# A mixture-of-experts block whose second expert stage writes its rows straight to the output

## The reference

```python
def ffn(x_):                                    # x_: 4096 x 128
    idx = argmax(x_ @ router.T, axis=-1)        # one of 8 experts for each token
    y  = down[idx] @ (silu(gate[idx] @ x_) * (up[idx] @ x_))           # 128 -> 256 -> 128
    ys = (silu(x_ @ w_gate_s.T) * (x_ @ w_up_s.T)) @ w_down_s.T        # the shared expert
    return y + ys

x = x + 0.5 * ffn(layernorm(x))
n = layernorm(x)
x = x + n + gate * circ_corr(decayed_sum(circ_conv(n, bind_key)), unbind_key)   # sum over earlier tokens
x = x + 0.5 * ffn(layernorm(x))
```

## Time and profile before

| | |
|---|---|
| median of 3 runs (lowest to highest) | 297.3 us (297.2 to 298.74) |
| the profiled execution | 297.33 us |
| its span | 295.6 us |
| TensorE busy | 254.9 us, 86% |
| TensorE weight loads | 211.0 us, 71% |
| VectorE busy | 189.0 us, 64% |
| ScalarE busy | 160.5 us, 54% |
| GpSimd busy | 178.7 us, 60% |
| mean DMA rate | 96 GB/s |

### The profile page before, as it was taken

One profiled execution on the slowest core, in us unless ns is written; L12 is line 12 of the kernel. 1 busy time (PEld: TensorE's weight loads), 2 busy tenths in 40 slices (PEclk: granted clock), 3 DMA queues, 4 the chain that ended last, 5 costly groups with the idle time before them and its releaser, 6 DMA issues.

```text
span 295.6 us, 6436 instructions
## 1 busy us (share of the span) xinstructions
PE 254.9 (86%) x1788; PEld 211.0 (71%) x1788; DVE 189.0 (64%) x734; ACT 160.5 (54%) x374; POOL 178.7 (60%) x260
## 2 busy tenths in 40 slices
PE   0799999969999999985589988999779999999940
PEld 0557777648999999845466767766369999999520
DVE  4695665864555555448996999867625566565362
ACT  2705545145767767326497877750447767775100
POOL 6555677722777777723457788877307758887400
PEclk9999999999999999997676999999999999999995
DMA  6970111323344321147000001112323434311297
GB/s 187 332 300 27 48 55 59 95 79 74 102 111 107 105 81 47 45 130 185 0 1 27 29 28 38 49 45 83 96 64 104 107 94 111 90 54 48 65 303 237
DMA packets 34996, 28.42 MB, mean 96 GB/s; under 512 B 4784, under 2 KB 31792, under 8 KB 34704
## 3 DMA queue, kind: packets, MB, share of 16 engines
q1 hardware_dynamic: 25328, 16.06, 19.7%
q0 software_dynamic: 4544, 9.45, 9.7%
q10 hardware_dynamic: 5088, 2.50, 2.9%
HBM read 15.37 MB, written 12.62 MB: 95 GB/s over the span
## 4 chain that ended last, share of the span: by engine, by line
POOL 33%; PE 22%; issue 19%; DMA 10%; DVE 9%; ACT 2%; SPq 2%; POOLq 0%; DVEq 0%; ACTq 0%
POOL dispatched L349 15%; POOL returned L378 12%; PE bank L951 10%; PE bank L959 4%; PE bank L874 4%; DMA ey<-returned 4%; POOL scale_f L338 2%; DMA xres<-in_x 2%; POOL token L372 2%; DMA dispatched<-xn,slot 2%; DMA returned<-ey,token 2%; DVE st_f L550 1%; DMA xs<-dispatched 1%; SPq L308 1%; PE bank L899 1%
## 5 line engine op out<-in xcount | busy, mean ns | idle before, releaser
L378 POOL DMA_INDIRECT returned<-ey,token x78 | 76.8, 985 | 32.8 <-issue 17.8
L951 PE MATMUL bank<-xsT,wgu 128*128 128x128 f32 x624 | 83.0, 276 | 2.4 <-ACT xsT L497 2.4
L349 POOL DMA_INDIRECT dispatched<-xn,slot x64 | 63.5, 992 | 24.6 <-issue 17.7
L951 PEld LDWEIGHTS bank<-xsT,wgu 128*128 128x128 f32 x624 | 75.7, 192 | 3.4 <-ACT xsT L497 1.7
L874 PE MATMUL bank<-xnT,gu 128*128 128x512 f32 x128 | 66.7, 649 | 3.6 <-DVE hs L623 2.8
L805 DVE COPY ey<-bank 128x128 f32<-128x128 f32 x78 | 22.7, 292 | 45.6 <-PE bank L959 45.6
L481 ACT ACTIVATE wgu<-gu 128x512 f32 x78 | 48.3, 623 | 4.1 <-issue 3.9
L454 ACT ACTIVATE sg<-bank 128x512 f32<-128x512 f32 x32 | 18.9, 592 | 54.7 <-PE bank L874 47.3
L959 PE MATMUL bank<-wdn,eh 128*128 128x128 f32 x312 | 47.5, 276 | 0.5 <-DVE eh L800 0.5
L503 ACT ACTIVATE eg<-bank 128x256 f32<-128x256 f32 x78 | 29.8, 383 | 32.6 <-PE bank L951 32.4
L959 PEld LDWEIGHTS bank<-wdn,eh 128*128 128x128 f32 x312 | 40.9, 192 | 0.9 <-DVE eh L800 0.9
(11 more groups left out here) (102 smaller groups left out, 282.7 us busy)
## 6 DMA issues: line engine op xcount, KB each, us to landing
xs<-dispatched SPq DMA_DIRECT2D x80, 66.0 KB, 1.9
ey<-returned SPq DMA_DIRECT2D x16, 256.0 KB, 5.7
gu<-in_gu SPq DMA_DIRECT2D x1, 2048.0 KB, 11.3
out<-xres ACTq DMA_DIRECT2D x8, 256.0 KB, 4.2
returned<-ey,token POOLq DMA_INDIRECT x78
dn<-in_dn SPq DMA_DIRECT2D x1, 1024.0 KB, 11.7
dispatched<-xn,slot POOLq DMA_INDIRECT x64, 2.3
dispatched<-pads SPq DMA_DIRECT2D x10, 66.0 KB
```

Of the source, the lines that this page charges most:

```text
L349: nc.gpsimd.indirect_dma_start(dispatched[:, :], bass.IndirectOffsetOnAxis(slot[:, i:i + 1], 0), xn[:, i, :], None, bounds_check=last_row) ...
L378: nc.gpsimd.indirect_dma_start(returned[:, :], bass.IndirectOffsetOnAxis(token[:, b:b + 1], 0), ey[:, b, :], None, bounds_check=last_back) ...
L951: last = nc.tensor.matmul(bank[4 + b % WR][:, i * P:(i + 1) * P], wgu[:, b % WR, i * P:(i + 1) * P], xsT[:, b // 2 % 2, b % 2, :], start=T ...
```

## The change

In stage 1 the dispatched row also carries the residual of its token. `xn` becomes 260 words wide, 132 as before and 128 that are now the storage of `xres`; `dispatched` becomes two tensors, one with rows of 132 words for stage 0 and one with rows of 260 for stage 1. In stage 1 the residual must be complete when it is dispatched, so all 24 shared parts are done before: a front step `k` does (k-1, 1), (k-1, `DOWN`) and (k, 0), there is one more step, `front(1, G)`, and `scatter(1, k-1)` is issued in step k, behind a wait for `half_done` of its group. VectorE does the first of the three parts ahead of `choose`, where it was behind. The evacuation of an expert block in stage 1 multiplies the product by 0.5 and adds the residual that came with the row; the indirect transfer writes to `out`. Rows of padding and repeated blocks are beyond the bound and not written. The read back, sums and stores of stage 1 are gone.

```diff
-    dispatched = nc.dram_tensor("dispatched", [E * CAP, ROW], F32, kind="Internal")
-    returned = nc.dram_tensor("returned", [DUMP * (E + 1), C], F32, kind="Internal")
+    dispatched = [nc.dram_tensor(f"dispatched{f}", [E * CAP, w], F32, kind="Internal")
+                  for f, w in enumerate((ROW, WIDE))]
+    returned = nc.dram_tensor("returned", [N, C], F32, kind="Internal")
+    home = [returned[:, :], out.rearrange("b t c -> (b t) c")]
...
-        xres = sb("xres", [P, NT, C])
-        xn = sb("xn", [P, NT, ROW])
+        xn = sb("xn", [P, NT, WIDE])
+        xres = xn[:, :, ROW:WIDE]
...
-        xs = sb("xs", [P, NBL, ROW])
+        xs = sb("xs", [P, NBL, WIDE])
+        ey = xs[:, :, ROW:WIDE]
+        back = ey
...
-        def parts_at(k, i):
-            return SHARED_PARTS[PER_STEP * (k - 1) + i:][:1] if 1 <= k < G else []
+        def parts_at(f, k, i):
+            if f == 0:
+                return SHARED_PARTS[PER_STEP * (k - 1) + i:][:1] if 1 <= k < G and i < PER_STEP else []
+            g, part = ((k - 1, 1), (k - 1, DOWN), (k, 0))[i]
+            return [(g, part)] if valid(g) and 0 <= k <= G else []
...
             def scatter(f, k):
                 pool.wait_ge(slotted, f * G + k + 1)
+                if f == 1:
+                    pool.wait_ge(half_done, G + k + 1)
                 for i in range(k * TPG, (k + 1) * TPG):
                     nc.gpsimd.indirect_dma_start(
-                        dispatched[:, :], bass.IndirectOffsetOnAxis(slot[:, i:i + 1], 0),
-                        xn[:, i, :], None, bounds_check=last_row).then_inc(sent, 16)
+                        dispatched[f][:, :], bass.IndirectOffsetOnAxis(slot[:, i:i + 1], 0),
+                        xn[:, i, 0:width(f)], None, bounds_check=last_row).then_inc(sent, 16)
...
-                if valid(k):
-                    scatter(1, k)
+                if valid(k - 1):
+                    scatter(1, k - 1)
...
                     nc.gpsimd.indirect_dma_start(
-                        returned[:, :], bass.IndirectOffsetOnAxis(token[:, b:b + 1], 0),
-                        ey[:, b, :], None, bounds_check=last_back).then_inc(blk_out, 16)
+                        home[f], bass.IndirectOffsetOnAxis(token[:, b:b + 1], 0),
+                        ey[:, b, :], None, bounds_check=last_back, oob_is_err=False).then_inc(blk_out, 16)
...
             # ScalarE, front(f, k); PE takes part i = 2 at the very end of its step
-                for g, part in parts_at(k, 1):
-                    shared(f, g, part)
+                for i in (1, 2):
+                    for g, part in parts_at(f, k, i):
+                        shared(f, g, part)
...
             # VectorE, front(f, k)
+                if f == 1:
+                    for g, part in parts_at(f, k, 0):
+                        shared(f, g, part)
                 if valid(k):
                     root = f == 0 and k == 2
                     choose(n, q, kind, later, later, root)
...
                 def evac_y(b):
                     dve.wait_ge(blk_dn, f * NB + b + 1)
-                    nc.vector.tensor_copy(ey[:, b, :], y_of(b)).then_inc(blk_y, 1)
+                    if f == 0:
+                        done = nc.vector.tensor_copy(ey[:, b, :], y_of(b))
+                    else:
+                        done = nc.vector.scalar_tensor_tensor(out=ey[:, b, :], in0=y_of(b), scalar=0.5,
+                                                              in1=ey[:, b, :], op0=ALU.mult, op1=ALU.add)
+                    done.then_inc(blk_y, 1)
...
             steps(middle, 4)
+            front(1, G)
             before_experts(1)
             experts(1)
-            for g, part in SHARED_PARTS[LATE:-1]:
-                shared(1, g, part)
-            for k in range(G):
-                add_back(1, k, x3_done)
-                if k == 2:
-                    shared(1, *SHARED_PARTS[-1])
```

More of the change, by code:

```diff
@@ L25 @@
 ROW = C + 4
+WIDE = ROW + C
 CAP = N + P
@@ L416, in _ @@
             steps(middle, 4)
+            scatter(1, G - 1)
             experts(1)
@@ L484, in before_experts @@
             def before_experts(f):
-                for g, part in SHARED_PARTS[EARLY:LATE - 1]:
+                for g, part in SHARED_PARTS[EARLY:LATE - 1] if f == 0 else []:
                     shared(f, g, part)
@@ L688, in front @@
                             newton_step(i)
-                for g, part in parts_at(k, 0):
-                    shared(f, g, part)
+                if f == 0:
+                    for g, part in parts_at(f, k, 0):
+                        shared(f, g, part)
                 if f == 1 and valid(k + 2):
@@ L907, in front @@
                     last.then_inc(mixed, 1)
-                for g, part in parts_at(k, 1):
+                for g, part in parts_at(f, k, 1):
                     shared(f, g, part)
@@ L929, in front @@
                     turn("a", k + 3, xa, 1 - q, x2_done)
+                for g, part in parts_at(f, k, 2):
+                    shared(f, g, part)
             def count_all():
@@ L965, in experts @@
                 turn_pair(0)
-                pe.wait_ge(half_done, f * G + parts_done(LATE, down=True))
-                pe.wait_ge(mult_done, f * G * HH + parts_done(LATE, down=False))
+                last = PARTS if f else LATE
+                pe.wait_ge(half_done, f * G + parts_done(last, down=True))
+                pe.wait_ge(mult_done, f * G * HH + parts_done(last, down=False))
                 gate_up_block(0)
@@ L997, in _ @@
             steps(lambda k: front(1, k), 3)
-            for g, part in SHARED_PARTS[EARLY:LATE]:
-                shared(1, g, part)
+            front(1, G)
             experts(1)
-            for g, part in SHARED_PARTS[LATE:]:
-                shared(1, g, part)
 def kernel(L0_attn_x, L0_attn_bind_key, L0_attn_unbind_key, L0_attn_gate, L0_attn_decay, L0_ffn_up, L0_ffn_gate,
```

53 lines of the change are left out of this document (25 added, 28 removed).

## The result

The changed kernel takes 310.4 us (median of 6 runs, 309.7 to 314.6), the kernel before 297.4 us on the same chip (6 runs, 296.8 to 299.0): 4.8% slower, ratio 1.048 with a 95% interval of 1.043 to 1.054. The forecast was 307.8 us, within 301 to 315. Executions over 1.5% above the fastest of the same kernel are left out of all ratios, and of the medians in the table of the experiments.

What follows compares the result with a forecast made beforehand. It took the kernel as bound by the stage 2 routing front, then TensorE in the experts, then a 16.8 us tail after the last expert row. Sum: 297.33 + 26.7 (front) + 0.6 (wide rows) - 16.8 (tail) = 307.8 us, range 301 to 315.

Steps and rivals of the forecast that it cites:

- The end: After the last expert row lands: read back, sums and stores go, removing 16.8 us; the last transfer lands in 2.25 us.
- The loop of 10.6 us: Stage 1 front: waits between ScalarE, VectorE and TensorE close a loop, making one full step 10.6 us.
- two changed orders: Stage 1 front: ScalarE's norm ahead of the second silu, VectorE's product ahead of `choose`; together they close the 10.6 us loop.
- The steps one by one: Stage 1 front: gate-up starts from 155.37 us to 224.2 us, the first gate-up at half clock costing 1.74 us.
- step 6: Stage 1 front step without `add_self`: forecast to take 8.2 us.
- the clock rival: Stage 1 front: TensorE's waits drop it to half clock, 312 us, or 318 with gate-ups slow too; chance 0.14.
- The last dispatch at 236.0: End of the front: the last transfer into `dispatched` starts at 236.0 us, was 209.30; the front gets 26.7 us longer.
- Wide rows: Landing and first read of a block: dispatched rows of 1040 bytes, were 528, add 0.6 us, between 0 and 0.9.
- GpSimd's time for wide rows: GpSimd's 0.97 us for each transfer into `dispatched`: taken as unchanged by wider rows, adding nothing.
- that rival: GpSimd pays for wide rows: its 0.97 us rise by half, 309.4 us, or double, 312.8 us; chance 0.08.
- The experts: Second expert stage: multiply-add in place of VectorE's copy out of PSUM, priced at nothing; stage stays at 58 us.
- The packed rival: Stage 1 front: the loop doesn't close, parts pack into idle time, last transfer starts at 226.7; 298.5 us, chance 0.12.

Runs made afterwards that it cites:

- e7: Kernel before with only the end changed: rows straight to the output, padding dropped, no read back, residual or last five shared parts; 283.6 us, ratio 0.953.
- e8: As e7, but rows go to the scratch tensor with none dropped, and the output gets one early store; 282.0 us, ratio 0.949.
- e3: Changed kernel with `choose` put back ahead of the product on VectorE, as before the change; 324.5 us, ratio 1.096.
- e4: Changed kernel with the edits of e2 and e3 together; 319.4 us, ratio 1.079.
- e12: Changed kernel with ten unread TensorE products added ahead of the second expert stage; 309.3 us, ratio 1.042.
- e1: The changed kernel run again, unaltered, for a second profile; 311.2 us, ratio 1.051 to the kernel before.
- e9: e5 with `add_self` moved right behind the norm of `xa` of the step before on ScalarE; 298.2 us, ratio 1.003.
- e2: Changed kernel with the second silu put ahead of `add_self` and the norm on ScalarE in stage 1; 302.9 us, ratio 1.021.
- e6: Changed kernel with two unread 128x512 products added ahead of each gate-up (k-1, 1) of stage 1; 314.5 us, ratio 1.058.
- e5: e2 with VectorE's product of (k-1, 0) moved behind the scan and read-back sum of the next step; 300.9 us, ratio 1.016.
- e10: e9 with ten unread TensorE products added ahead of the second expert stage; 296.9 us, ratio 1.002.
- e11: e10 with gate-up (7, 0) ahead of group 6's down part, and the last down part and sum in halves; 297.1 us, ratio 1.002.

## Why the prediction was right, and where its sizes were off

**The end** (16.8 us removed): right in kind, 2.2 us too large. It took the landing of 2.25 us for all that follows the last transfer; in the changed kernel, e7 and e8 it is 4.4 us, because GpSimd's closing drain ends 2.1 us after the landing. That term was left out of the sum.

**The loop of 10.6 us**: the steps from 154.82 us on measured 10.55, 10.55, 10.55, 10.27 and 9.80 us, where 10.6, 10.6, 10.6, 10.3 and 9.8 were forecast, the half clock apart. Each link was where it was put, to within 0.15 us: silu at + 1.92, second silu + 5.97 for 6.07, product + 6.63 for 6.70, `add_retrieved` and transposes to 10.55. But one sentence behind it was wrong. It said that two changed orders close the loop, and only ScalarE's is shown as a cause; VectorE's product ahead of `choose` is the better order (e3, e4). The links were read rightly; what the old order would cost in their place was never worked out.

**The steps one by one**: the sum from the first gate-up to that of group 7 was forecast as 68.8 us and is 68.8 (154.82 to 223.63), but by two errors that cancel. The half clock was put at the first gate-up, as in the earlier trace rows; in this profile it didn't fall there, and fell at the down product of step 6 in its place (forecast 8.2 us, measured 9.93), with TensorE's clock in these two stretches:

```profile
209.00:212.40 3.40, 2.01 (x11) 1.24 (x9) 1.42 (x3) 2.63 (x7) 2.39 (x3) 0.99 0.15 55
212.40:216.00 3.60, 3.60 (x18) 3.60 (x19) 1.03 (x6) 0.00 (x0) 1.57 (x2) 0.53 0.27 96
```

In the first profile, of the execution of 314.64 us, it fell at the first gate-up and in two down products (3.29 and 3.12 us), and the last transfer into `dispatched` started at 239.46 us. In e12's profile it fell at the first gate-up and at no down product. So the clock rival came true in part: not in each step, but once to three times in the front, at 1.1 to 2.0 us each. Its upper price of 1.8 us for a down product holds: 1.1 to 1.6 us here, up to 1.74 in e3 and e4. Whether it is what spreads the runs was not tested.

**The last dispatch at 236.0**: 236.13. The sum was forecast at 232.0 and was done at 231.5, and GpSimd started 0.79 us after it, where 0.16 was taken. Transfers of 1.27 us each, as forecast.

**Wide rows** (+ 0.6 us): 0.5 us up to the first block, nothing up to the first product. SP reads the first block 2.68 us after the start of the last transfer (2.58 before), a block of 130 KB lands in 2.2 us for 1.9, and TensorE starts on the first block 4.97 us after that transfer for 4.44 before (4.9 to 5.2 in all ten kernels with wide rows). But the first product stands behind the transposes of two blocks, and in the kernel before the second block came late, 5.66 us after the transfer:

```profile
213.74 0.30 PE L940 MATMUL bank<-ident,xs 128*128 128x128 f32 x1 [0.53 <-DMA xs<-dispatched]
214.96 0.33 PE L940 MATMUL bank<-ident,xs 128*128 128x128 f32 x1 [0.92 <-DMA xs<-dispatched]
```

In e1 both transposes run one behind the other from 241.10 us. So the first product comes 6.58 us after the transfer for 6.66. The forecast's term had the right size and was hidden by a wait that it didn't look at; why the second block came late before isn't shown.

**GpSimd's time for wide rows**: taken as flat, and flat. The count of packets came out as forecast, 48 for 32 a transfer, but not by the forecast's working. The trace's packet records of GpSimd's queue have sizes: in the kernel before 1024 packets of 4224 bytes, 1248 of 4096 and 2272 of 4, so for each transfer and DMA engine one packet with all eight rows (8 x 528 or 8 x 512 bytes) and one of 4 bytes, and not "four 528-byte rows a packet". In e1's trace the wide rows are 1024 packets of 4160 bytes, four rows each. The Trainium skill (DMA: Bandwidth & Descriptors, section SWDGE vs HWDGE vs iDMA) has 4096 bytes as the preferred most in a packet; these packets are larger, so this trace doesn't keep to it. By that preference eight wide rows would have taken three packets of data, and they took two: that the count fitted is luck. The time on GpSimd didn't go by packets, 0.97 us at both sizes; that rival is refuted by the rows.

**The experts** (nothing): the multiply-add takes 292 ns and the copy in stage 0 291, as forecast. The stage is 1.5 us longer because its first 16 products ran at half clock, 3.75 us for 2.02 before; in e12, where they ran at full clock, the way from the first product to the last transfer out is 60.24 us for 62.07, and 60.60 before. That was a price missing from the forecast: TensorE now stands still for 10.33 us ahead of the stage, since no shared parts are left to lie there.

**The packed rival** (298.5 us, chance 0.12): not what the changed kernel does, but what the same change can do. e9, with its three orders undone or moved, takes 298.2 us with a last dispatch at 223.2. The rival said 226.7; that the time agrees to 0.3 us is luck, since an earlier dispatch and an end 2.2 us and experts 1.6 us longer than it took nearly cancel.

## What to carry to other kernels

When a result moves from the end of a kernel into the middle, add up not the moved work but the turn that each in-order engine makes with the new order. Here the moved parts are 8.7 us of TensorE and the front grew by 26.8, of which three reorderings gave back 12.9. And before an order is blamed, price the other one: a wait of 2 us ahead of a product can cost more through the clock behind it than through itself. A tail that is cut short bounds the whole gain (14 to 15 us here), and it can be measured by itself before the work that pays for it is written.

## What the runs showed of the hardware that was not expected

- TensorE's clock behind a wait. The profiles of the changed kernel (both), e2, e3, e4, e6, e9 and e12 have 64 down products in the front of stage 1. Behind a wait of less than 1 us, none of 26 was slow (1.95 to 2.05 us); behind 1.74 to 1.81 us, 2 of 17 (3.29 and 3.57 us); behind 2.03 to 2.22 us, 9 of 10 (2.54 to 3.79 us). Behind 1.39 to 1.41 us it was 2 of the 3 that had logits ahead of the wait (3.12 and 3.64 us), and none of the 8 that had a gate-up ahead of it. e5, e10 and e11 have 24 more, 21 behind less than 1 us and 3 behind 1.41 with a gate-up ahead, and none was slow. The nine slow ones behind more than 2 us are all of e3 and e4, so this is a count and no rule.
- Ten 128x512 products ahead of the expert stage kept the full clock for its first products in one kernel (2.02 us) and not in another (3.57 us).
- 4.4 us pass from the start of a last indirect transfer of GpSimd to the end of the span, whether its rows are dropped or not, though a reader waits only 2.25 us for it. GpSimd's closing drain ends 4.23 us after that start in all 14 profiles.
- For each DMA engine eight rows of 528 bytes go in one packet of 4224 bytes, eight of 1040 in two of 4160, each time with one of 4 bytes beside them. It costs GpSimd nothing: its transfers take 986 to 1002 ns on average in the ten kernels with wide rows, 992 before.
- A dropped row still moves 4 bytes: in e7, 90 packets of GpSimd's queue have 32 bytes in place of 4096, 4 for each of eight rows, and its transfers to the output take GpSimd 982 ns on average, for 985 before.
- GpSimd's first transfer of group 7 starts 0.79 us after VectorE's sum is done (e1), against 0.30 us between one transfer and the next.
